# A fused attention and FP8 kernel on one core: the first eight row tiles and the first two units in a hand-written order

## What is computed

```
q  = rope(rmsnorm(xn @ Wq + bq, qn_w));  lk = rope(rmsnorm(xn @ Wlk + blk, kn_w));  lv = xn @ Wlv + blv
w_cmp   = softmax over each group of 4 rows of (xn @ Wcmp + bcmp)        # the "logits"
entries = sum over each group of 4 rows of w_cmp * xn                    # 256 per sequence
ck = rope(rmsnorm(entries @ Wk + bk, kn_w));  cv = entries @ Wv + bv     # compressed keys, values
sparse = softmax over the 8 largest q.ck (causal) @ cv                   # per head
local  = softmax over the last 128 to 256 positions of q.lk @ lv         # per head, banded
attention = (sparse + local) / 2 @ Wo + bo
ffn = fp8(xn * scale) / scale @ (fp8(W2 * scale1) / scale1)
```

## Time and profile before

| | us |
|---|---|
| median of three runs | 2481.17 |
| the profiled execution, whole | 2483.7 |
| its span, first to last instruction | 2481.9 |
| PE busy in the span | 2452.2 |
| DVE, POOL, ACT busy | 2003.0, 1807.3, 1660.7 |

### The profile page before, as it was taken

The page is one execution under the profiler, slowest core; times in us unless marked ns, Lnnn a source line. Parts: engine busy times, 40 slices in busy tenths (PEclk is TensorE's granted clock), DMA queues, the critical chain, the costliest instruction groups (busy, mean ns, idle before and its releaser), DMA issues. The chain is left out here.

```text
span 2481.9 us, 55994 instructions
## 1 busy us (share of the span) xinstructions
PE 2452.2 (99%) x15452; PEld 2174.4 (88%) x15452; DVE 2003.0 (81%) x6638; ACT 1660.7 (67%) x4818; POOL 1807.3 (73%) x3214
## 2 busy tenths in 40 slices
PE   7999999999999999999999999999999999999999
PEld 6888888888888888888888888888888888888888
DVE  7788888888788878788778887888878878888786
ACT  5667676777666766666666666666766666666666
POOL 6787787776787767777768776677777876666765
PEclk9999999999999999999999999999999999999999
DMA  5433133333342232332442323333145213222201
GB/s 160 136 107 113 62 118 115 118 109 116 126 124 62 78 96 57 70 84 69 148 147 70 91 62 74 96 58 91 53 141 166 95 58 101 64 72 94 87 17 56
DMA packets 189818, 233.42 MB, mean 94 GB/s; under 512 B 23875, under 2 KB 107589, under 8 KB 189509
## 3 DMA queue, kind: packets, MB, share of 16 engines
q1 hardware_dynamic: 188932, 229.58, 31.5%
q10 hardware_dynamic: 576, 0.26, 0.0%
HBM read 163.70 MB, written 65.03 MB: 92 GB/s over the span
## 5 line engine op out<-in xcount | busy, mean ns | idle before, releaser
L1777 POOL TENSOR_TENSOR t<-raw,tB 128x128 f32<-128x128 f32 x512 | 226.3, 463 | 528.0 <-DVE raw L1311 528.0
L1120 ACT ACTIVATE ch<-bVC,blT 128x128 fp32r<-128x128 f32 x510 | 159.9, 365 | 536.4 <-PE bVC L840 535.9
L739 PE MATMUL bQK<-wh,xh 128*128 128x512 f32 x1024 | 424.4, 414 | 0.0
L740 PE MATMUL bQK<-wl,xh 128*128 128x512 f32 x1024 | 403.8, 394 | 0.0
L741 PE MATMUL bQK<-wh,xl 128*128 128x512 f32 x1024 | 401.3, 392 | 0.0
L1721 POOL TENSOR_TENSOR r<-ss,mh 128x4 f32<-128x4 f32 x256 | 287.9, 1125 | 58.6 <-DVE ss L1319 56.1
L758 PE MATMUL bVC<-wh,xh 128*128 128x256 f32 x1020 | 309.0, 303 | 0.0
L1347 DVE CUSTOM_DVE_ANT_0 P<-bS,cst 128x256 f32<-128x256 f32 (+1 forms) x512 | 204.3, 399 | 124.4 <-PE bS L790 119.1
L1087 ACT ACTIVATE P<-P,nm,r 128x256 f32<-128x256 f32 (+1 forms) x512 | 295.3, 583 | 0.0
L760 PE MATMUL bVC<-wh,xl 128*128 128x256 f32 x1020 | 288.3, 283 | 0.0
L759 PE MATMUL bVC<-wl,xh 128*128 128x256 f32 x1020 | 287.8, 282 | 0.0
(11 more groups left out here) (236 smaller groups left out, 7633.6 us busy)
## 6 DMA issues: line engine op xcount, KB each, us to landing
wh<-kept SPq DMA_DIRECT2D x144, 256.0 KB, 4.1
wl<-kept SPq DMA_DIRECT2D x144, 256.0 KB, 4.5
kept<-wh SPq DMA_DIRECT2D x48, 256.0 KB, 3.2
kept<-wl SPq DMA_DIRECT2D x48, 256.0 KB, 3.4
woh<-kepto SPq DMA_DIRECT2D x48, 256.0 KB, 3.4
wol<-kepto SPq DMA_DIRECT2D x48, 256.0 KB, 4.1
ini<-in_hidden_states SPq DMA_DIRECT2D x24, 256.0 KB, 3.6
xs<-xsh SPq DMA_DIRECT2D x24, 256.0 KB, 2.6
```

Source lines behind the costliest of these rows:

```text
L739: e.matmul(bQK[:, :], a, b, start=kt == 0, stop=False)
L740: e.matmul(bQK[:, :], a, bl, start=False, stop=False)
L1777: last = e.tensor_tensor(t2[:, :, :, d_], raw[:, u % 2, :, :, s_], tB[:, :, u % 8, d_].unsqueeze(1).broadcast_to([128, 2, 2, 32]), ALU.mult)
```

## The change

Nothing that is computed changes. The steps -8 to 1 are reordered on four engines, and two buffers are swapped:

- DVE makes the FP8 scales (`isc`) one step later; POOL takes each tile's power one step earlier, ahead of a weight split.
- ACT copies the row `Wcmp` into PSUM (`bP[0]`) once, and DVE's logits of tiles 1 to 7 read it from there.
- PE issues 40 fills first and 3 after each `turn_x` and each `logits`; the 24 fills of step 1 and the 6 before are gone.
- The steps 0 and 1 are written out by hand on PE, ACT and DVE. The first block's projection goes behind half a projection of unit 0, in bank `bVC`; tile 7 is transposed into `bP[0]`; `entries(6)` stands in step 1.
- Block 1's `turn_ck`, `hi_ck` and `lo_ck` (step 5) stand behind the scores and values of the step on PE, behind `hi_c` on ACT and behind `lo_c` on DVE, where they stood ahead of them.

```
-        "lo": (2, 2, 3, 3), "max": (2, 2, 3, None), "ew": (3, 3, 4, None), "wm": (3, 3, 4, None), "et": (3, 4, 8, None),
+        "lo": (2, 2, 3, 3), "max": (2, 2, 3, None), "ew": (3, 3, 4, None), "wm": (3, 3, 4, None), "et": (3, 3, 8, None),
...
+        def turned_x(t):
+            return bP[0] if t == LAST_FIRST else bT
+        def kv_of(k):
+            return (bY if k else bVC)[:, 0:256]
...
             def turn_x(t):
                 e.wait_ge(S["xn"], t + 1)
-                if free["T"]:
+                if t == LAST_FIRST:
+                    e.wait_ge(S["wl"], t + 1)
+                elif free["T"]:
                     e.wait_ge(S[free["T"][0]], free["T"][1])
...
# PE
+            e.wait_ge(S["ones"], 1)
+            fill(40)
             e.wait_ge(S["d_c"], 16)
             for s in range(FIRST, 0):
                 if tile_at(s, "turn") is not None:
                     turn_x(tile_at(s, "turn"))
+                    fill(3)
                     logits(tile_at(s, "turn"))
+                    fill(3)
                 if tile_at(s, "et") is not None:
                     entries(tile_at(s, "et"))
-                if block_at(s, "kv") is not None:
-                    ckv(block_at(s, "kv"))
-                if s in (-3, -2):
-                    fill(3)
-            for s in range(NU):
+            proj_qk(0, 0)
+            ckv(0)
+            turn_x(6)
+            logits(6)
+            entries(5)
+            proj_qk(0, 1)
+            proj_qk(1, 0)
+            turn_x(7)
+            logits(7)
+            turn_ck(0)
+            entries(6)
+            proj_qk(1, 1)
+            tr(0)
+            proj_v(0)
+            for s in range(2, NU):
+                k, late = block_at(s, "turn"), s < 8
                 if u0 is not None:
                     proj_qk(u0, 0)
-                if block_at(s, "turn") is not None:
-                    turn_ck(block_at(s, "turn"))
+                if k is not None and not late:
+                    turn_ck(k)
...
                 if tile_at(s, "max") is not None:
                     logits(tile_at(s, "max"))
+                if k is not None and late:
+                    turn_ck(k)
...
# ACT
             e.activation(junk[:, 0:1], mh[:, 0:1], ACT.Exp)
+            e.wait_ge(S["d_g"], 16 * 2)
+            e.activation(bP[0][:, :], wcb[:, :], ACT.Copy)
...
+            exp_w(5)
+            put_kv(0)
+            hi_x(6)
+            cast_x(6)
+            put_et(5)
+            exp_w(6)
+            squares(0)
+            diagonal(7)
+            hi_x(7)
+            hi_ck(0)
+            put_et(6)
+            kscale(0)
+            cast_x(7)
+            hi_qk(0)
+            squares(1)
+            put_v(0)
+            kscale(1)
...
# DVE
-                e.tensor_tensor_reduce(junkd if t < NL else junke, xs, wcb[:, :], 1.0, bcm[:, 0:1], ALU.mult, ALU.add,
+                if 1 <= t < FIRST_TILES:
+                    e.wait_ge(S["dg"], 1)
+                row = bP[0] if 1 <= t < FIRST_TILES else wcb
+                e.tensor_tensor_reduce(junkd if t < NL else junke, xs, row[:, :], 1.0, bcm[:, 0:1], ALU.mult, ALU.add,
...
-                if s == FIRST + 1:
+                if s == FIRST + 2:
                     e.wait_ge(S["d_s"], 16 * 2)
                     e.tensor_scalar(isc[:, 2:4], isc[:, 0:2], 0.5, None, ALU.mult, ALU.bypass)
...
+            normalise(7)
+            weights4(5)
+            group_max(6)
+            lo_cv(0)
+            rope_ck(0)
+            put_qk(0)
+            lo_x(6)
+            weights4(6)
+            sum_qk(0)
+            rope_add(0)
...
+            group_max(7)
+            lo_ck(0)
+            neg_r(0)
+            put_qk(1)
+            lo_x(7)
+            lo_qk(0)
+            sum_qk(1)
+            rope_add(1)
...
                 if u4 is not None:
                     lo_c(u4)
+                if k is not None and late:
+                    lo_ck(k)
...
# POOL
-                if s < 0 and tile_at(s, "power") is not None:
-                    power_x(tile_at(s, "power"))
+                if s == FIRST:
+                    power_x(0)
+                if s < 0 and tile_at(s + 1, "power") is not None:
+                    power_x(tile_at(s + 1, "power"))
```

More of the change, by code:

```diff
@@ L751, in proj_v @@
                 dst = new_v(u)
+                if u == 0:
+                    e.wait_ge(S["lo_cv"], 1)
                 if i == 0:
@@ L798, in turn_p @@
                         e.wait_ge(S["pl"], u)
+                    elif h == 0:
+                        e.wait_ge(S["lo_x"], FIRST_TILES)
                     for n in range(nloc(u) // 128):
@@ L928, in ckv @@
                     e.wait_ge(S["nb"], 1)
+                else:
+                    e.wait_ge(S[free["Y"][0]], free["Y"][1])
+                    free["Y"] = ("lo_cv", k + 1)
                 for kt in range(KT):
-                    e.matmul(bY[:, 0:256], et[:, kt, :], wkv[:, kt, :], start=kt == 0, stop=False)
-                e.matmul(bY[:, 0:256], minus1[0:1, :], bkv[:, :], start=False, stop=True).then_inc(S["kv"], 1)
-                free["Y"] = ("lo_cv", k + 1)
+                    e.matmul(kv_of(k), et[:, kt, :], wkv[:, kt, :], start=kt == 0, stop=False)
+                e.matmul(kv_of(k), minus1[0:1, :], bkv[:, :], start=False, stop=True).then_inc(S["kv"], 1)
             def turn_ck(k):
@@ L1147, in cast_x @@
                     e.wait_ge(S["isc"], 2)
-                e.activation(a8[:, slot8(t), :], bT[:, :], ACT.Copy, scale=isc[:, 0:1], saturate=False)
-                e.activation(b8[:, slot8(t), :], bT[:, :], ACT.Copy, scale=isc[:, 2:3],
+                e.activation(a8[:, slot8(t), :], turned_x(t)[:, :], ACT.Copy, scale=isc[:, 0:1], saturate=False)
+                e.activation(b8[:, slot8(t), :], turned_x(t)[:, :], ACT.Copy, scale=isc[:, 2:3],
                              saturate=False).then_inc(S["b8"], 1)
@@ L1230, in run_scalar @@
                     put_et(tile_at(s, "et"))
-                if block_at(s, "put") is not None:
-                    put_kv(block_at(s, "put"))
-            for s in range(NU):
+            exp_w(5)
[15 more added lines that the diff above has]
+            kscale(1)
+            for s in range(2, NU):
                 u0, u1, u2, u3, u4 = (unit_at(s, lag) for lag in range(5))
+                k, late = block_at(s, "hi"), s < 8
                 if tile_at(s, "ew") is not None:
@@ L1238, in run_scalar @@
                     exp_4(tile_at(s, "share"))
-                if block_at(s, "hi") is not None:
-                    hi_ck(block_at(s, "hi"))
+                if k is not None and not late:
+                    hi_ck(k)
                 if tile_at(s, "hi") is not None:
@@ L1603, in run_vector @@
                     lo_x(tile_at(s, "lo"))
[L1604 to L1608, removed]
+            normalise(7)
[8 more added lines that the diff above has]
+            rope_add(0)
+            e.wait_ge(S["d_3"], 32)
+            e.tensor_scalar(blT[:, :], blT[:, :], 0.5, None, ALU.mult, ALU.bypass).then_inc(S["bl"], 1)
+            group_max(7)
[6 more added lines that the diff above has]
+            rope_add(1)
+            for s in range(2, NU):
                 u0, u1, u2, u3, u4, u5 = (unit_at(s, lag) for lag in range(6))
-                if block_at(s, "lo") is not None:
-                    lo_ck(block_at(s, "lo"))
+                k, late = block_at(s, "lo"), s < 8
+                if k is not None and not late:
+                    lo_ck(k)
                 if u2 is not None:
```

34 lines of the change are left out of this document (13 added, 21 removed).

## The result

| | before | after |
|---|---|---|
| median of the comparison, us | 2481.07 (2480.66 to 2482.46, 9 runs) | 2488.79 (2485.04 to 2491.09, 9 runs) |
| profiled execution, us (span) | 2483.7 (2481.9) | 2486.41 (2484.6) |
| ratio of after to before | | 1.0029, 95% interval 1.002 to 1.0037 |

The change makes the kernel 7.7 us **slower** in the medians, where 5.5 us faster was forecast. The two profiled executions lie only 2.7 us apart. The runs of after also scatter over 6 us, those of before over 2.

A forecast was written before the change was run, and what follows sets the result against it. PE, busy 2452.2 of 2481.9 us, was taken as the bound. A front 7.5 us earlier and 1.9 us lost in step 5 gave -5.6, taken as -5.5: 2475.7 us, range 2471.5 to 2480.0.

The forecast's parts named there:

- What bounds, and where the change acts: Whole kernel: PE works 2452.2 of 2481.9 us; the change touches only the first steps, through PE's earlier start or added waits.
- Scales later, power sooner; logits 0.75: First tiles on DVE: tile 0 at 7.5, tile 1 at 10.25, logits from PSUM at 0.75 us each.
- So DVE is through at 30.6: Front, end of tile 5's `lo_x` on DVE: reached at 30.6 us, 5.9 us earlier.
- The cover here is PE: Before the first `put_qk`: PE's listed work ends near 36.0 at its upper level, 1.2 us ahead of need.
- From the first `put_qk` to the landmark: Stretch from the first `put_qk` to `proj_qk(2)`: 6.4 us of PE work instead of 9.5, a gain of 3.1.
- the landmark: Start of `proj_qk(2)`, marking the end of the front: forecast at 44.3 instead of 51.83, 7.5 us earlier.
- about 1: Step 2, entries 7: PE arrives earlier and waits about 1 us for `wm`, with a net effect of 0.
- Block 1's keys: Step 5: saves PE's 1.74 us wait, but `tr(4)` waits 3.6 us for `lo_ck(1)`; net +1.9 us.
- Rival 1: First tiles: PE becomes the bound at its lower clock level, 4.8 us a tile, end near 2487; chance 0.04.
- The sum: Whole kernel: -7.5 us at the front plus 1.9 in step 5 gives -5.6, taken as -5.5.

The follow-up runs named there:

- c_after: The change run again unaltered as a control, against the kernel before: +6.8 us, ratio 1.0026.
- e5: The change with the parking DMAs of tiles 0 and 1 issued ahead of the loads of chunks 4 and 5: +2.2 us over before, ratio 1.0009.
- e8: e6 plus 24 fills (for 3) in PE's wait for tile 1's logits and 8 before step 2's `entries(7)`: -6.1 us against before, ratio 0.9973.
- e6: The change with the edits of e1, e2 and e5 together: -5.6 us against before, ratio 0.9978.
- e7: The change with the edits of e1 and e2, without the moved parking: -0.8 us against before, ratio 0.9996.
- e2: The change with `ckv(0)` put back ahead of the first half of `proj_qk(0)`: +4.4 us over before, ratio 1.0016.
- e1: The change with block 1's keys put back ahead of step 5's scores on PE, ACT and DVE: +3.5 us over before, ratio 1.0015.
- b1: The kernel before with only block 1's keys moved late in step 5: +3.8 us over before, ratio 1.0013.
- e3: The change with 24 fills instead of 3 behind the logits of tile 0: +5.4 us over before, ratio 1.0023.
- e4: The change without the three fills behind each `turn_x` and each `logits`, the 40 at the start kept: +5.8 us over before, ratio 1.0022.

## Why the prediction was wrong

- **What bounds, and where the change acts**: right. 6.3 us of the loss are there by `tr(5)`, 7.0 by `tr(21)`.
- **Scales later, power sooner; logits 0.75**: right in the profile of after, tile 0 at 7.56 for 7.5, tile 1 at 10.50 for 10.25, all seven PSUM logits 0.75 us. In this the trace agrees with the rule that the prediction named (the Trainium skill, SBUF — State Buffer, Who interferes with whom: one SBUF input does not contend with GpSimd): the one at 11.07 lay wholly inside a subtraction of POOL of 1.50 us from 10.66, and took 0.75. Tile 1 was partly luck: in c_after, the same kernel, it began at 11.95, as late as in seven of the twelve profiles with the scales moved (last section); the prediction gave the moved scales 0.36 us and no collision with POOL.
- **"So DVE is through at 30.6"**: the first step that failed. `lo_x(5)` ended at 35.0. The sum followed DVE's rows only. From tile 1 to the end of `lo_x(5)` it had 30.6 - 10.25 = 20.3 us; after took 24.5, e5 with the parking moved 22.3, and e8 with the upper clock besides 20.0 (these rows, then their tile 1 at 10.50, 11.85 and 11.93):
```profile
34.29 0.69 DVE L1507 TENSOR_TENSOR xl<-bT,xh 128x512 fp32r<-128x512 f32 x1
```
```profile
33.43 0.69 DVE L1509 TENSOR_TENSOR xl<-bT,xh 128x512 fp32r<-128x512 f32 x1
```
```profile
31.28 0.68 DVE L1511 TENSOR_TENSOR xl<-bT,xh 128x512 fp32r<-128x512 f32 x1
```
So some 2 us are the parking DMA, queued behind SyncE's loads, and some 2 are PE's clock. The DMA set `cast_x(4)` at 29.5, near where it was before, and with it `lo_x(4)`, tile 5 on PE, and POOL's last power (`st` came 1.95 us late, tables done at 38.6 for 36.3). The word "parking" is not in the prediction. Its price in medians is 5.5 us (e5), or 4.8 (e6 against e7).
- **"The cover here is PE"**: the second. The prediction listed PE's entries, half projection and keys and ended them at 36.0 at the upper level. It never asked who waits behind the keys. `put_et(4)` had to, with `exp_w(5)` and tile 7's logits behind it on ACT, for 6.52 us. And PE was at 1.2 GHz. The first `put_qk` was done at 46.6 for 37.9. Price of the order: 3.3 us (e2) or 4.3 (e7 against e1).
- **From the first `put_qk` to the landmark**: right, 6.5 us for 6.4. `entries` of tile 7 waited 1.08 for "about 1", but the 1.2 us of the clock behind that wait were not in the sum.
- **Block 1's keys**: the wait was right, 3.88 us for 3.6, and net 2.1 for 1.9 in the change, by DVE's list as worked out. Its clock was missed: behind the wait PE ran 3.4 us at 1.2 GHz. Price together: 4.2 us (e1), or 3.8 measured alone (b1), for 1.9.
- **Rival 1**: its mechanism appeared (4.2 us per tile for its 4.8, PE fully busy at 1.2 GHz from 12 to 29) and its 2487 is near the profiled 2486.4, but it is a part of the loss and not the whole. In e3 the clock was up for most of the tiles and `cast_x(4)` stood at the DMA all the same, so in the change the clock's 2 us lay mostly under that wait; e8 against e5 shows them. It got 0.04. The 40 fills did raise the clock at first: granted 0.98 from 7 to 12, and 0.63 us for the four transposes of tile 0, which take 1.09 in before. That is as the Trainium skill's page TensorE: Matmul & The Clock Gate, Part 1: The HAM clock gate, has it of activity. PE then idled from 10.2 to 12.8, and the clock fell at 11.8. The prediction weighed only whether it would rise, not whether it would stay.
- **The sum**: -7.5 + 1.9, where the profile of after has +6.3 by `tr(5)`. Of the 11.9 us between, 8.8 are the landmark (53.07 for 44.3), 1.8 lie between it and `tr(3)`, most of them the clock of step 2, and 1.3 are step 5 with its clock. With the three losses taken out, the version measures -5.6 (e6) and -6.1 (e8). The first is the forecast's number by chance: for this version, which has no late keys, the forecast would be -7.5. What supports the size of the front's gain is the trace of e8: its first `put_qk` is done at 39.1 and its landmark comes at 45.6, with tile 1 1.7 us later than forecast; less that, 37.4 and 43.9 for 37.9 and 44.3. So the gains were sized about right, and the losses left out.

## What to carry to other kernels

When an engine's work is moved earlier, list every wait that its followers have on other queues, with the time at which each is satisfied now: one that shows no idle time may be met a microsecond ahead of need, as the parking DMA was. When an instruction is put behind another in an explicit order, look for who overwrites what it reads, and what stands behind that on its own engine. And a wait of 1 to 4 us that is put into a matmul stream is priced with what PE may lose afterwards at 1.2 GHz, here 1.1 to 2.3 us behind each wait after which the clock fell.

## What was not expected of the hardware

- The granted clock of before reads 1.00 up to 36.9, where its transposes take what they take in after under a granted 0.50 (1.06 and 1.09 us). Such a record is checked against durations.
- Whether the clock falls behind a short wait differs between executions. The 1.08 us wait at step 2's `entries` stands in all nine profiles of the change and of its variants without fills there. Behind it the clock fell for 3.4 us in after, e1, e3, e4 and e6, and not in c_after, e2, e5 and e7; after and c_after are one kernel. That fits the change's wide scatter, but no run isolated it.
- A 128x1 `tensor_tensor` of the scales on DVE took 0.38 to 0.43 us in five profiles and 1.25 in seven, though nothing of it differs but its start beside POOL's 128x512 work. In after and in c_after:
```profile
9.94 0.16 DVE L1634 TENSOR_SCALAR isc<-isc 128x2 f32<-128x2 f32 x1
10.00 0.16 DVE L1635 RECIPROCAL sm<-isc 128x2 f32<-128x2 f32 x1
10.20 0.38 DVE L1637 TENSOR_TENSOR isc<-sm 128x1 f32<-128x1 f32 x1
```
```profile
10.12 0.57 DVE L1634 TENSOR_SCALAR isc<-isc 128x2 f32<-128x2 f32 x1
10.59 0.15 DVE L1635 RECIPROCAL sm<-isc 128x2 f32<-128x2 f32 x1
10.78 1.25 DVE L1637 TENSOR_TENSOR isc<-sm 128x1 f32<-128x1 f32 x1
```
POOL's `wh` began at 9.95 and 10.04: in one case just after DVE's first instruction, in the other just before it. The second then started behind POOL's `wl` (10.75) and waited it out. A tenth of a microsecond decides over 1.4 us of tile 1 (10.50 or 11.95): moving the scales put them into POOL's way. In the five fast profiles DVE's first instruction began from 0.07 us before to 0.01 after POOL's `wh`, in the seven slow ones 0.03 to 0.09 after it.
